# One subtraction of the first stage moved from VectorE to GpSimd, with the waits it needs there

## The reference, cut to what matters

```
x = L0_attn_x
mod = (_silu(L0_c) @ L0_wmod).reshape(L0_c.shape[0], 6, 1, -1)
sa, ca, ga, sb, cb, gb = (mod[:, 0], mod[:, 1], mod[:, 2], mod[:, 3], mod[:, 4], mod[:, 5])
...
h = _layernorm(x, axis=-1) * (1 + ca) + sa
# inside the attention:
q = (x @ Wq + bq).reshape(b, s, H, HD).transpose(0, 2, 1, 3)
k = (x @ Wk + bk).reshape(b, s, H, HD).transpose(0, 2, 1, 3)
v = (x @ Wv + bv).reshape(b, s, H, HD).transpose(0, 2, 1, 3)
...
x = x + ga * _L0_attn_ref(h, ...)
h = _layernorm(x, axis=-1) * (1 + cb) + sb
x = x + gb * _L0_ffn_ref(h, ...)
```

## Time and profile before

| | |
|---|---|
| median of three runs | 2058.83 us |
| the profiled execution | 2059.94 us |
| its span, first to last instruction | 2058.1 us |
| first stage | 0 to 129.66 us |
| busy in the span: TensorE matmul / VectorE / ScalarE / GpSimd | 1825.8 / 465.4 / 1336.0 / 290.5 us |
| chunk loop, 60 to 110 us, per 10 us: TensorE / VectorE / ScalarE / GpSimd | 10.00 / 9.79 / 7.1 to 7.2 / 0.00 us |

### The profile page before, as it was taken

One profiled execution on the slowest core, in us unless ns is written; L12 is line 12 of the kernel. 1 busy time (PEld: TensorE's weight loads), 2 busy tenths in 40 slices (PEclk: granted clock), 3 DMA queues, 4 the chain that ended last, 5 costly groups with the idle time before them and its releaser, 6 DMA issues. The chain is left out here.

```text
span 2058.1 us, 47091 instructions
## 1 busy us (share of the span) xinstructions
PE 1825.8 (89%) x18425; PEld 948.7 (46%) x18426; DVE 465.4 (23%) x1368; ACT 1336.0 (65%) x1649; POOL 290.5 (14%) x333
## 2 busy tenths in 40 slices
PE   4944999999999989999999997674699999999995
PEld 3832333333333333333333332563376767676663
DVE  4954000000000000000000000545233333333331
ACT  3723899998999989999999997221233333333331
POOL 1000100001100011000111000456112121212111
PEclk8975999999999999999999999766799999999998
DMA  4464400004000040000000000962412221222223
GB/s 138 155 156 112 89 10 18 10 2 89 17 10 10 10 88 18 10 9 10 17 18 18 2 2 27 333 245 88 118 33 33 33 33 31 34 33 33 33 33 97
DMA packets 84274, 116.10 MB, mean 56 GB/s; under 512 B 9484, under 2 KB 76108, under 8 KB 83532
## 3 DMA queue, kind: packets, MB, share of 16 engines
q1 hardware_dynamic: 67064, 90.97, 15.8%
q0 software_dynamic: 13296, 17.80, 5.1%
q10 hardware_dynamic: 3760, 5.03, 0.9%
HBM read 73.03 MB, written 40.74 MB: 55 GB/s over the span
## 5 line engine op out<-in xcount | busy, mean ns | idle before, releaser
L1112 ACT ACTIVATE at_probs<-at_scores 128x1536 f32<-128x1536 f32 (+2 forms) x756 | 1022.5, 1436 | 55.5 <-PE at_scores L1013 50.2
L1013 PE MATMUL at_scores<-at_q_rows,kept_k_rows 99*32 99x512 bf16 (+3 forms) x9920 | 618.0, 362 | 32.8 <-ACT at_probs L1112 17.0
L1030 PE MATMUL at_out<-at_probs,kept_v 128*17 128x512 f32 (+3 forms) x4832 | 588.5, 566 | 5.0 <-DVE at_out_T L1125 4.7
L1013 PEld LDWEIGHTS at_scores<-at_q_rows,kept_k_rows 99*32 99x32 bf16 x9920 | 239.4, 96 | 557.4 <-ACT at_probs L1112 344.3
L1819 ACT ACTIVATE ex_hT<-ex_ps_hT,kept_b 128x128 f32<-128x128 f32 x568 | 154.1, 382 | 374.7 <-PE ex_ps_hT L1776 374.7
L1784 PE MATMUL ex_ps_y<-kept_w,ex_hT 128*128 x1136 | 258.7, 381 | 2.5 <-ACT ex_hT L1819 2.5
L1765 PE MATMUL ex_ps_h<-kept_w,ex_xT 128*128 x568 | 259.6, 600 | 1.0 <-DVE ex_xT L1834 0.9
L1125 DVE COPY at_out_T<-at_out 128x512 f32<-128x512 f32 x32 | 22.1, 692 | 969.7 <-PE at_out L1030 969.7
L1097 POOL TENSOR_SCALAR_AFFINE_SELECT at_probs<-at_probs 128x512 f32<-128x512 f32 (+2 forms) x156 | 83.0, 541 | 1006.8 <-ACT at_probs L1112 1004.9
L1784 PEld LDWEIGHTS ex_ps_y<-kept_w,ex_hT 128*128 128x128 f32 x1136 | 211.5, 191 | 28.8 <-issue 2.7
L1030 PEld LDWEIGHTS at_out<-at_probs,kept_v 128*17 128x17 f32 x4832 | 128.1, 98 | 129.9 <-DVE at_out_T L1125 20.2
(11 more groups left out here) (220 smaller groups left out, 965.3 us busy)
## 6 DMA issues: line engine op xcount, KB each, us to landing
kept_w<-in_W SPq DMA_DIRECT2D x16, 1024.0 KB, 10.8
ex_x_tile<-queue SPq DMA_DIRECT2D x72, 129.5 KB, 2.0
k_parts<-kparts SPq DMA_DIRECT2D x8, 768.0 KB, 3.7
q_parts<-qparts SPq DMA_DIRECT2D x8, 768.0 KB, 3.7
at_q_rows<-q_parts SPq DMA_DIRECT2D x32, 192.0 KB
kept_k_rows<-k_parts SPq DMA_DIRECT2D x4, 1120.0 KB
x_rows<-in_x SPq DMA_DIRECT2D x4, 1024.0 KB, 13.7
kept_k_rows<-k_parts SPq DMA_DIRECT2D x8, 512.0 KB
```

Source lines behind the costliest of these rows:

```text
L1013: ins = nc.tensor.matmul(ps_s[b:b + CT, c % 2, at:at + part], k_rows[:, k + b:k + b + CT], q_rows[:, q:q + part], start=True, stop=True)
L1030: ins = nc.tensor.matmul(ps_o[h * CT:h * CT + HD + 1, first:C], v[:, kb, g * GH + h, :], probs[:, slot, column:column + width], start=i == ...
L1112: nc.scalar.activation(probs[:, c % RING, 0:width], ps_s[:, c % 2, 0:width], ACT.Exp).then_inc(exped, 1)
```

## The change

The function `split_low` and its calls leave VectorE's list. The same subtraction, with the same two waits and the same semaphore, stands as a loop over the eight chunks at the end of GpSimd's list for this stage. Who waits for it (TensorE, by `low_ready`) stays as it was, and so does the single buffer.

```diff
@@ gpsimd
             pool.wait_ge(pool_step, 10 + 2 * KD)
 
+            for c in range(NC):
+                u = c % 2
+                pool.wait_ge(h_ready, (c + 1) * KD)
+                if c > 0:
+                    pool.wait_ge(k_ready, 2 * c)
+                nc.gpsimd.tensor_tensor(hT_low[:, 0], hT[:, u], hT_high[:, u], ALU.subtract).then_inc(low_ready, 1)
+
@@ vector
-            def split_low(c):
-                u = c % 2
-                dve.wait_ge(h_ready, (c + 1) * KD)
-                if c > 0:
-                    dve.wait_ge(k_ready, 2 * c)
-                nc.vector.tensor_tensor(hT_low[:, 0], hT[:, u], hT_high[:, u], ALU.subtract).then_inc(low_ready, 1)
-
             rows = bv_rows[:].rearrange("p (h d) -> p h d", h=H)
-            split_low(0)
             for c in range(NC):
                 split(c, 0, kf, kparts, k_stored)
-                if c + 1 < NC:
-                    split_low(c + 1)
                 split(c, 1, qf, qparts, q_stored)
```

## The result

The kernel after takes 1.0027 of the time before, with a 95% interval of 1.0015 to 1.0038: medians of 2062.77 us and 2057.64 us over 13 runs each, 5.1 us apart. A later series of the same two kernels gave 1.0025 (1.0014 to 1.0035). It is slower, by about 0.26%.

What follows compares the result with a forecast made beforehand. VectorE, its lap 9.97 us against TensorE's 9.81, was taken to set the first stage's end. Last split 116.70 + 0.6 + 15.0 = 132.3 against 125.47, plus semaphore waits: +7.0, median 2065.8, range 2062 to 2071.

Steps and rivals of the forecast that it cites:

- The take-away: First stage: eight subtractions leave VectorE, seven in the loop at 1.14, 7.98 us; the idle 0.70 goes too.
- The start: Chunk 0: TensorE waits 1.14 us more for GpSimd's subtraction; 0.6 taken, 1.1 if the clock's rise moves along.
- The blocked time: Chunk loop: GpSimd's subtractions hold VectorE, five laps at 2.04 and two at 2.41, 15.0 us.
- The values read PSUM and are not held: Chunk loop: VectorE's values (L453) read PSUM, so GpSimd's subtraction does not block them; 1.13 us each.
- The sum: First stage: 116.70 + 0.6 + 15.0 = 132.3 for the last split, 6.8 us later; forecast +7.0.
- a wait on two semaphores: First stage: GpSimd's wait costs 0.1 in each lap that it shifts, some 0.2 to 0.4 us in all.
- Casts wait too: VectorE's splits: casts out of SBUF are taken to wait for GpSimd as two-input subtractions do.
- The casts pass: Rival, first stage: GpSimd covers one 0.73 us cast in most laps; +4.2, 2063.0 us; chance 16%.
- VectorE keeps the lock: Rival, first stage: VectorE's next instruction goes ahead of waiting GpSimd; 16.9 blocked, +12.0, 2070.8 us; chance 12%.
- Beside the values: Rival, first stage: GpSimd starts as VectorE's values start; 9.0 blocked, +0.8, 2059.6 us; chance 8%.
- no exclusion: Rival, first stage: GpSimd reads beside VectorE, TensorE bounds the lap at 9.81; 1.3 us earlier, 2057.5; chance 9%.
- Every later stage keeps its length: Sign in the profile: the first stage's end moves from 129.66 to about 136.7, later stages unchanged.

Runs made afterwards that it cites:

- e3: The kernel after, with the subtraction of chunk 0 alone put back on VectorE: ratio 1.0012 to before, first stage ends at 136.17 us.
- e4: The kernel after, with the subtractions of chunks 1 to 7 left out, GpSimd only counting the semaphore: ratio 0.9991 to before, first stage ends at 130.39 us.
- e5: The kernel after, with GpSimd subtracting only half the columns in chunks 1 to 7: ratio 0.9997 to before, first stage ends at 131.29 us.
- e2: The kernel after, unchanged, profiled and timed again: ratio 1.0025 to before, first stage ends at 136.89 us.
- e1: The kernel before, unchanged, profiled and timed again: ratio 1.0000, first stage ends at 130.89 us.
- e8: The kernel after, with eight tiny memsets added on VectorE ahead of the loop: ratio 1.0021 to before, score stage 62.11 us.
- e9: The kernel before, with eight tiny memsets added on GpSimd: ratio 0.9991 to before, score stage 64.24 us.
- e6: The kernel after, with GpSimd writing zeros by memset in place of the subtraction in chunks 1 to 7: ratio 0.9989 to before, first stage ends at 129.56 us.

## Why the prediction was right

The forecast was +7.0 and slower; measured were +5.1 between the medians, slower. Step by step:

- *The take-away* held. All eight subtractions left, the idle 0.70 too, and VectorE has no idle time in the late laps.
- *The start.* The first split began 1.34 later (48.45 against 47.11), where 0.6 was taken and 1.1 was the bound. TensorE got fast about 1.3 later too, so it looks as if the rise had moved along; but the clock's rise moves by more than that between executions of one kernel, so this term can't be tested (e3).
- *The blocked time* was the step that decides, and it held. The seven stretches are 2.14, 2.04, 2.03, 2.06, 2.06, 2.05 and 2.04, together 14.42, against 15.0. The five settled laps were taken at 2.04, and that this fits to 0.02 is partly luck: two sizes behind it were off and cancel. The full price of a hold isn't 2.41. A held cast ends 0.55 after GpSimd does, though alone it takes 0.69, and a held subtraction 1.08 after, for 1.23; so a hold costs what is left of GpSimd's instruction less 0.15, at most some 2.2. (The 0.06 of L1586 was the end of the held instruction, not a cost added to it: it lost 1.79 - 0.19 = 1.60 of the 1.73 that GpSimd had left.) And in the last four laps GpSimd starts later than thought, 0.25 before the end of the values and not 0.45 (91.92 against 90.95 + 1.22), since from their end to its next start, at 102.81, are 10.64 us and not 10.42. The first two laps, taken at 2.41, are shorter for the first of these reasons, and because VectorE's next instruction was issued a little after GpSimd had begun (51.17 after 51.10 in the first).
- *The values read PSUM and are not held*: so it is. GpSimd starts inside them in the late laps and takes its plain 2.36, and they take their 1.22.
- *The sum*: 1.34 - 0.70 - 7.98 + 14.42 = 7.08 for the stage; its end moved by 7.05, to 136.71, where about 136.7 was forecast. The lap is 10.89, forecast 10.9. The lap is the test of the mechanism; that the stage's end fits to 0.05 is luck. The start was 0.74 more than taken, the blocked time 0.58 less, and no run shows the 0.2 to 0.4 added for a wait on two semaphores: GpSimd starts 0.08 after the end of `hT` in each lap, and the sum closes without it. And the repeats of the two kernels are 6.00 apart, not 7.05.
- *Casts wait too* was taken from one instance, and it is so: in four laps of the seven it is the first cast of the keys that waits. "The casts pass" is out.
- *VectorE keeps the lock* is out: at 60.90 GpSimd waited 0.34 and had its turn at the next boundary, at 61.38. VectorE's next instruction needs the result of the last and was issued 0.04 after it, so who would win with both ready isn't shown. "Beside the values" and "no exclusion" are out by the stretched instructions themselves. e4 and e5 show the price by its size: no GpSimd instruction, no price; half of one, less than half of the stretch, and nothing in the laps that TensorE bounds.
- *"Every later stage keeps its length"* failed. The score stage is 2.2 to 2.7 shorter in after and e2 than in before and e1, with a barrier ahead of the attention of 0.5 for 2.8 (in e8, with the short barrier too, it is 1.0 to 1.3 shorter). 7.05 - 2.65 = 4.4 in the first pair of profiles and 6.00 - 2.24 = 3.8 in the second are 0.18 to 0.21%, inside both measured intervals. The forecast of the total, +7.0, had nothing for this, which is why it lies above the 5.1 measured. Why code in the first stage changes that barrier is open; e8 and e9 exclude the number of instructions.
- *Two readings of rows* were loose, without harm: by the code L1348 adds and L1586 multiplies, where the prediction speaks of a subtraction or comparison. Both have two inputs in SBUF, which is what the argument needs.

The two profiled executions ended at the same time because the attention and the experts took 2.80 and 2.12 less in the one of after, on top of the score stage; the attention alone varies by 6 us over the profiles. A single pair of spans would have shown no change at all.

## What to carry to other kernels

Ahead of giving VectorE's work to an idle GpSimd, add up how long VectorE is held for it: here 2.05 us against 1.14 saved, seven times, though in those seven laps nobody waited for GpSimd's result. An engine that is idle isn't free if its instruction holds up the other's. Effects of a few tenths of a per cent are read from the stage's own end and lap, and then from many timed runs, never from two spans.

## What the runs showed of the hardware

A held instruction of VectorE shows as a long one, not as idle time ahead of it, and ends a fixed time after GpSimd's: 0.54 to 0.56 us for a cast of 128x1024 and 1.08 to 1.10 for a subtraction, behind a GpSimd instruction of about 2.4 (after and e2), 1.3 to 1.4 (e5) or, for the cast, 0.95 (e6). And a memset of GpSimd, which reads nothing, lets a subtraction of VectorE pass and holds a cast.

The clock column of these profiles has to be read with care. Windows of a stretch in which TensorE does nothing, in before and in after, then one of after in which it works:

```profile
25.00:30.00 5.00, 0.00 (x0) 0.00 (x0) 4.41 (x15) 0.00 (x0) 0.00 (x0) 0.50 0.00 0
```
```profile
25.00:30.00 5.00, 0.00 (x0) 0.00 (x0) 4.44 (x14) 0.00 (x0) 0.00 (x0) 1.00 0.00 0
45.00:46.00 1.00, 1.00 (x4) 0.81 (x3) 0.00 (x0) 0.00 (x0) 0.00 (x0) 1.00 0.00 0
```

TensorE's pairs in after, in and behind that last window:

```profile
45.34 1.05 PE L352 MATMUL ps_k<-hT_high,wk_low 128*128 128x512 f32 x2
46.20 0.85 PE L352 MATMUL ps_k<-hT_low,wk_high 128*128 128x512 f32 x2
...
47.67 0.71 PE L352 MATMUL ps_q<-hT_high,wq_high 128*128 128x512 f32 x2
```

The pair at 45.34 took 1.05, as at the lower level, under a column of 1.00. The clock wasn't ahead of the matmuls: the first stretch that the trace of after records for the clock begins at 46.65, at the upper level, where that of before begins at 21.50, and the column reads 1.00 where nothing is recorded. From 46.65 on the pairs are fast. So a stage's speed is better read from its matmuls than from that column alone, and the mean clock of a whole span (0.941 in after, 0.934 in before) holds this gap too.

The same code got its upper clock at 45.4 in one execution and at 48.1 in another, and the stage ended 1.2 us later in the second.
